# Third layer's aggregation with products of 256 columns in place of 512

## The reference

```python
h = jnp.maximum(_layernorm(x, axis=-1), 0.0)
x = x + _L2_gnn_ref(h, edge_index, L2_gnn_W, L2_gnn_b)

def _L2_gnn_ref(x, edge_index, W, b):
    ...
    src = jnp.concatenate([edge_index[0], loops])
    dst = jnp.concatenate([edge_index[1], loops])
    deg = jax.ops.segment_sum(jnp.ones_like(dst, dtype=x.dtype), dst, num_segments=n)
    dinv = jnp.where(deg > 0, jax.lax.rsqrt(deg), jnp.zeros_like(deg))
    norm = dinv[src] * dinv[dst]
    h = x @ W
    msg = h[src] * norm[:, None]
    out = jax.ops.segment_sum(msg, dst, num_segments=n) + b
    return jax.nn.relu(out)
```

## Time and profile before

| | us |
|---|---|
| median of 3 runs | 1010.93 |
| lowest and highest | 1009.24, 1012.62 |
| the profiled execution | 1009.79 |
| its span, from the first to the last instruction | 1008.3 |
| TensorE busy in the span | 980.9 |
| VectorE, ScalarE, GpSimd busy | 673.6, 431.0, 125.6 |
| granted clock of TensorE, mean | 0.995 |

### The profile page before, as it was taken

The page is one execution under the profiler, slowest core; times in us unless marked ns, Lnnn a source line. Parts: engine busy times, 40 slices in busy tenths (PEclk is TensorE's granted clock), DMA queues, the critical chain, the costliest instruction groups (busy, mean ns, idle before and its releaser), DMA issues.

```text
span 1008.3 us, 14745 instructions
## 1 busy us (share of the span) xinstructions
PE 980.9 (97%) x5170; PEld 812.3 (81%) x5170; DVE 673.6 (67%) x1252; ACT 431.0 (43%) x654; POOL 125.6 (12%) x160
## 2 busy tenths in 40 slices
PE   6899989999999999999999999999999999999997
PEld 4688878888888888888888888888888888888885
DVE  6888797798788779454476333316436664988886
ACT  5588774544554557211152223224222223444543
POOL 2011310000000001233321000001110000333331
PEclk9999999999999999999999999999999999999999
DMA  7256390000000005554434111153451130101223
GB/s 249 85 186 224 114 275 1 0 22 1 0 21 0 0 0 115 130 215 167 166 125 137 52 42 42 40 190 104 146 188 69 68 120 1 42 22 63 83 84 121
DMA packets 27326, 93.42 MB, mean 93 GB/s; under 512 B 3530, under 2 KB 3530, under 8 KB 27136
## 3 DMA queue, kind: packets, MB, share of 16 engines
q1 hardware_dynamic: 16400, 58.07, 16.4%
q0 software_dynamic: 10880, 34.74, 11.3%
HBM read 64.48 MB, written 33.56 MB: 97 GB/s over the span
## 4 chain that ended last, share of the span: by engine, by line
PE 88%; DVE 6%; ACT 2%; issue 2%; DMA 1%; SPq 1%; ACTq 0%; DVEq 0%
PE ps L581 32%; PE ps L2040 12%; PE ps L1960 9%; PE ps L1962 9%; PE ps L1961 9%; PE ps L2013 4%; PE ps L2012 4%; PE ps L564 3%; DMA gb<-in_L_gnn_gate_b 1%; PE ps L1855 1%; PE ps L1811 1%; PE ps L1883 1%; PE ps L1814 1%; PE ps L1885 1%; PE ps L1827 1%
## 5 line engine op out<-in xcount | busy, mean ns | idle before, releaser
L1960 PE MATMUL ps<-g_hi,mask_hi 128*128 128x512 f32 x400 | 157.9, 395 | 4.3 <-DVE mask_lo L1502 4.2
L1962 PE MATMUL ps<-g_hi,mask_lo 128*128 128x512 f32 x400 | 156.5, 391 | 0.0
L1961 PE MATMUL ps<-g_lo,mask_hi 128*128 128x512 f32 x400 | 156.2, 390 | 0.0
L581 PE MATMUL ps<-w_hi,hT_hi 128*128 128x512 f32 x320 | 126.3, 395 | 0.0
L547 ACT ACTIVATE hT_hi<-ps 128x1024 fp32r<-128x1024 f32 x40 | 41.0, 1026 | 198.9 <-PE ps L564 198.9
L581 PE MATMUL ps<-w_lo,hT_hi 128*128 128x512 f32 x320 | 124.7, 390 | 0.0
L1097 ACT ACTIVATE mask<-ps,v 128x640 f32<-128x640 f32 x80 | 63.4, 794 | 113.7 <-PE ps L1962 53.5
L2040 PE MATMUL ps<-y_all,att_hi 128*128 128x512 f32 x400 | 109.9, 392 | 0.3 <-DVE att_lo L1681 0.3
L581 PE MATMUL ps<-w_hi,hT_lo 128*128 128x512 f32 x320 | 98.6, 389 | 0.0
L1960 PEld LDWEIGHTS ps<-g_hi,mask_hi 128*128 128x128 f32 x400 | 75.5, 189 | 22.0 <-issue 3.4
L1962 PEld LDWEIGHTS ps<-g_hi,mask_lo 128*128 128x128 f32 x400 | 75.4, 188 | 16.1
(11 more groups left out here) (196 smaller groups left out, 1833.3 us busy)
## 6 DMA issues: line engine op xcount, KB each, us to landing
xin<-x_after SPq DMA_DIRECT2D x30, 512.0 KB, 3.4
xres<-x_after POOLq DMA_DIRECT2D x20, 512.0 KB, 4.2
x_after<-xres POOLq DMA_DIRECT2D x20, 512.0 KB, 3.0
w_raw<-in_L_gnn_W SPq DMA_DIRECT2D x8, 1024.0 KB, 8.0
x_after<-g POOLq DMA_DIRECT2D x20, 256.0 KB, 7.3
xres<-x_after SPq DMA_DIRECT2D x10, 512.0 KB, 3.4
xin<-in_x SPq DMA_DIRECT2D x9, 512.0 KB, 3.4
out_x<-xres SPq DMA_DIRECT2D x9, 512.0 KB, 2.6
```

The lines of the kernel that those rows point to most:

```text
L581: last = nc.tensor.matmul(PRODUCT[d.n][b][:, half * BANK:(half + 1) * BANK], left[:, k, :], right[:, k, half * BANK:(half + 1) * BANK], st ...
L1960: nc.tensor.matmul(SUMS[dd], mask_hi[k][:, cols], g_hi[:, s, :], start=(s == 0), stop=False)
L1961: nc.tensor.matmul(SUMS[dd], mask_hi[k][:, cols], g_lo[:, s, :], start=False, stop=False)
L1962: last = nc.tensor.matmul(SUMS[dd], mask_lo[k][:, cols], g_hi[:, s, :], start=False, stop=(s == T - 1))
```

## The change

In `gcn_pe`, the loop over the two halves of the features becomes a loop over four quarters. Each pair of matmuls, with `y_hi` and with `y_lo`, now has 256 columns, and two sums stand side by side in a bank. Since `start` works on the whole bank, only the first quarter in each bank has it; the second quarter's first product finds its columns cleared. `skip_group_check` only switches off an inspection of such sums at build time. The block that runs for large counts, `low_pe`, stays with 512 columns.

```diff
                     left = ring[k][:, j * P:(j + 1) * P]
-                    for n in range(2):
-                        out_n = sums[j][:, n * BANK:(n + 1) * BANK]
-                        nc.tensor.matmul(out_n, left, y_hi[s][:, n * BANK:(n + 1) * BANK], start=(s == 0), stop=False)
-                        last = nc.tensor.matmul(out_n, left, y_lo[s][:, n * BANK:(n + 1) * BANK], start=False, stop=(s == T - 1))
+                    for n in range(4):
+                        cols = slice(n * BANK // 2, (n + 1) * BANK // 2)
+                        nc.tensor.matmul(sums[j][:, cols], left, y_hi[s][:, cols], start=(s == 0 and n % 2 == 0), stop=False,
+                                         skip_group_check=True)
+                        last = nc.tensor.matmul(sums[j][:, cols], left, y_lo[s][:, cols], start=False, stop=(s == T - 1),
+                                                skip_group_check=True)
```

## The result

The changed kernel takes 1016.33 us (median of 4 runs, 1015.81 to 1017.44), the kernel before in the same session 1010.09 us (4 runs, 1008.89 to 1012.62). The ratio is 1.0058 with a 95% interval of 1.0046 to 1.0069: slower by more than the 0.3% that the prediction set as its bound, where it had forecast no change. The time is the one that rival 1 gave, a fee for each matmul: 1016.3 us. The profiled execution took 1017.44 us with a span of 1015.9.

A forecast was written before the change was run, and what follows sets the result against it. TensorE, busy without a hole in the stage, was taken as the bound: span 1008.3 us, minus 0.3 for 800 matmuls at 113 ns, plus 1.5 around it gave 1009.5 profiled; plus 1.1 for the median, 1010.6 us, range 1008.5 to 1017.5.

The forecast's parts named there:

- rival 1: Third layer's aggregation: the 13.4 ns are a fee for each matmul, stage 96.1 us, +5.4, 1016.3 us; chance 0.20.
- The 13.4 ns: Aggregation stage: time between starts beyond streaming 512 columns, read as loss by length; 112.7 ns at 256 columns.
- the straight line: Distance between starts from 55.7 ns at 128 columns to 226.7 at 512, giving 112.7 ns at 256.
- 3.0 us bound: Whole kernel: about 0.3%, the least difference that a measurement can tell from no change.
- Rival 2: Aggregation stage: the weight load comes to the surface, 150.4 us, +59.7, or without overlap 174.2, +83.5; chances 0.09 and 0.01.
- The sequencer and the code: Aggregation stage: 480 more instructions keep TensorE fed and cost 0; two fetches, should they show, +1.3 us.
- Nobody who waits for the stage: ScalarE's count copies and VectorE's reading of sums: 0.3 us of room shrinks by 0.2 us at most, nothing opens.
- to 0.1 us: All stages other than the third layer's aggregation should keep their length to 0.1 us.

The follow-up runs named there:

- m3_curve: Kernel of matmul streams only, no network: eleven more sizes from 224 to 504 columns; 4-byte distances follow 0.4427 ns x columns + 3.3 ns.
- e5: Kernel before, with each 512-column product of the third layer's aggregation split into 264 and 248 columns: 1013.48 us against 1010.72, ratio 1.0030.
- e4: Kernel before, third layer unchanged, with the attention's 600 matmuls of 512 columns split into 1200 of 256: 1017.42 us, ratio 1.0063.
- m4_lock: Kernel of streams only, no network: sizes mixed in turn and fewer weight columns; 264 and 248 in turn 233.4 ns a pair, 256 repeated 120.0.
- m1_sizes: Kernel of streams only, no network: one stream for each size; 4-byte 226.7 ns at 512 columns, 120.0 at 256; bf16 215.7 and 109.2.
- e3_384_128: Third layer's aggregation with each 512-column product split into 384 and 128, against the kernel before: 1033.9 us, ratio 1.0227.
- e2_other_banks: Changed kernel with its four quarters in the order 0, 2, 1, 3: one run of 1016.3 us, stage 96.85 us.
- e1_half: Changed kernel with only the second half of the features split, two products of 512 and four of 256: 1014.38 us, ratio 1.0032 to the kernel before.

## Why the prediction was wrong

**The sum, as the runs have it.** 400 products, 13.3 ns dearer each, are 5.3 us. By the line of m3_curve one product of 512 columns would take 230.0 ns and two of 256 would take 2 x 116.6 = 233.3. Of the 13.3 ns, then,
- 3.3 are the fixed part of one more matmul, by the line;
- 6.7 are the fixed distance that 256 columns fall into, 2 x 3.4 (e5 takes it away);
- 3.3 are the good distance that 512 columns had and that is lost (e4's stage had it only in part, and paid less).

The parts are read off the line, which the single sizes meet to 1 or 2 ns, and add up to what was measured by construction; what tests them is e5, which has the first and the third, 6.6 ns, and measured 3.07 / 400 = 7.7 ns. The kernel's order, two of 264 and two of 248, lies between the two of them in turn (m4_lock, 233.4 ns a pair, 6.7 above 226.7) and each of them repeated (m3_curve, 120.2 + 114.8 = 235.0, 8.3 above). Why a repeated 248 stands above the line is not shown.

**The step that failed** is "The 13.4 ns". Its excess was held to be a loss by length, "in bf16 as in 4-byte numbers". Both supports were wrong. First, the 389 ns of bf16 were the duration of a matmul alone, which lasts some 11 ns longer than one in a stream; in a stream it is 379, and there the bf16 durations have no loss by length (379, 326, 272 and 219 ns for 512, 384, 256 and 128 columns in m1_sizes, one column in each cycle of 2.4 GHz). Second, the straight line was drawn between a bf16 point and a 4-byte point. The two types have lines of their own: 0.4167 ns x columns + 2.5 and 0.4427 ns x columns + 3.3. The step's idea was right in half: of the 13.4 ns at 512 columns most does go with the columns (512 x 0.026 = 13.3 by the slopes, less the 3.3 of the good distance, plus 3.3 of fixed part). But the size of 256 was taken where there was no row of its type, and is 120.0, not 112.7. Even a correct line would have given 116.6, +2.6 us (2 x 116.6 - 226.7 = 6.5 ns for each of 400), just under the 3.0 us bound; the rest needed a measured point at 256.

**Against rival 1 I counted** "the bf16 one of 512 columns lasts just as long, and those of 90 and 128 columns show nothing of it". This compared across types and read a duration for a distance. The rival's other line, that this type was never seen short, should have weighed more than 0.20. Its price of 120.1 ns came out to 0.1 ns and its stage of 97.0 us to 0.2. That is not luck as far as it goes, for 512 and 256 columns are two of the four sizes whose streams have the same 13.3 ns above their columns. As a mechanism for every matmul it did not hold: by it 264 columns would take 123.4 ns and 448 would take 200.1, and they take 120.2 and 202.5.

**What held.**
- TensorE alone sets the stage: busy in all of it before and after, so that each ns of distance arrived in the time.
- The load needs 111 ns between starts and was not the limit: m1_sizes and e3_384_128 both show it. Rival 2 did not come; loads of 128 rows overlap with matmuls on the same 128 rows from end to end of the stage.
- The sequencer and the code cost nothing: q8 carried 30 packets (the page's row above), one more than in the earlier trace rows, and there is no hole in the stage.
- Sharing a bank, the prediction's silent assumption, is free: the stage has the same 120.0 ns as the streams of m1_sizes with one sum in a bank, and in e2_other_banks the order of the banks changes nothing.
- Nobody who waits for the stage became late. The other stages kept their lengths except for the scatter ahead of the stage, 2.2 us in this pair of profiles, which the prediction's "to 0.1 us" had not allowed for.

**What is open.** Why four of the repeated sizes stand at 13.3 ns above their columns and not on the line. The runs show what breaks it (another size now and then, or fewer than 128 weight columns), and that short matmuls or transposes ahead do so for a while; they do not show the cause. The 64-weight-column streams show that 256 columns can also gain. Nor is it shown why 512 and 256 side by side lie above the line, 6 ns a pair in turn, and more in e1_half for the 512s. No version here beats the kernel before: each split adds the fixed part of a matmul at least, and 512 columns are what a bank holds.

## What to carry to other kernels

A price for a matmul is a distance between starts in a stream of that type, that number of columns and that number of weight columns; neither a duration nor a point of another type stands for it, and where the trace has no such row, the bounds deserve as much weight as the middle. In a stage that TensorE fills, splitting a 4-byte matmul of 512 columns cost 11.5 to 13.3 ns for each split when the halves were equal, and 7.7 when they were 264 and 248. If columns must be split, keep each piece above 248 or so, below which the load of 128 4-byte weight columns, 111 ns, is the price.

## What the runs showed of the hardware that was not expected

- 4-byte matmuls stream at 17 cycles for 16 columns plus 3.3 ns, most sizes within 1 ns, the exceptions of the next point and 248 and 272 columns (1.7 and 1.6 above) aside; bf16 at one cycle a column plus 2.5 ns.
- Repeated alike with 128 weight columns, 512, 384, 320 and 256 columns take 226.7, 173.3, 146.7 and 120.0 ns, each 13.3 above its columns at 2.4 GHz: 512 stands 3.3 below that line, 256 stands 3.4 above; 264 columns take 120.2. In e1_half, with pairs of 512 and of 256 mixed, the 512s take 231 to 235.
- A 4-byte load of 128 weight columns lasts 188 to 192 ns but may start every 111 ns; room beside a long neighbour is not used for a short one. With 64 weight columns 128 columns stream at 59.9 ns.
- 4-byte and bf16 matmuls in turn cost some 17 ns a pair over the sum of both.
- Alone, each waiting for the one before, matmuls of 512 columns last 390 ns in bf16 and 502 in 4-byte numbers, where they last 379 and 389 in a stream.
